# Layer L2 of a four-layer attention kernel: scores from projected queries and raw keys, with the key bias carried by the fully connected product and brought as a row by two transfers

## What is computed

```python
q = x3 @ Wq + bq                  # 256 -> 256
k = ctx @ Wk + bk                 # 128 -> 256
v = ctx @ Wv + bv
scores = softmax(q @ k.T / 16)    # per batch entry, 128 x 128
x4 = x3 + scores @ v
# fc before it:  x3 = x2 + layernorm(x2) @ fc_W + fc_b  (gain and bias of the norm folded in)
```

## Time and profile before

| | |
|---|---|
| median of 3 runs | 590.14 us (589.99 to 591.93) |
| the profiled execution, its own time | 591.77 us |
| its span from first to last instruction | 590.0 us |
| PE busy | 98% |
| POOL, DVE, ACT busy | 86%, 78%, 76% |
| granted TensorE clock, mean | 0.995 |
| DMA | mean 75 GB/s |

### The profile page before, as it was taken

The page is one execution under the profiler, slowest core; times in us unless marked ns, Lnnn a source line. Parts: engine busy times, 40 slices in busy tenths (PEclk is TensorE's granted clock), DMA queues, the critical chain, the costliest instruction groups (busy, mean ns, idle before and its releaser), DMA issues.

```text
span 590.0 us, 16396 instructions
## 1 busy us (share of the span) xinstructions
PE 576.3 (98%) x4752; PEld 562.4 (95%) x4752; DVE 461.0 (78%) x1442; ACT 449.5 (76%) x1534; POOL 505.6 (86%) x704
## 2 busy tenths in 40 slices
PE   6999999999999999999999999999999999999995
PEld 6898999999999999999999999999999999999984
DVE  2486888996888878887887779778778778967975
ACT  4679878678697777977985977968788888686663
POOL 5889999799898969988897899898959979994763
PEclk9899999999999999999999999999999999999999
DMA  8961112121312132221122224112230110000012
GB/s 255 367 209 37 56 46 92 46 77 61 98 47 82 46 106 85 82 63 65 47 64 64 72 62 138 46 28 94 70 100 11 56 46 20 2 3 0 21 36 91
DMA packets 29799, 44.06 MB, mean 75 GB/s; under 512 B 2704, under 2 KB 21520, under 8 KB 29712
## 3 DMA queue, kind: packets, MB, share of 16 engines
q1 hardware_dynamic: 29712, 43.02, 22.4%
HBM read 34.62 MB, written 8.39 MB: 73 GB/s over the span
## 4 chain that ended last, share of the span: by engine, by line
PE 90%; DVE 4%; issue 2%; ACT 1%; DMA 1%; SPq 1%; DVEq 0%; ACTq 0%
PE bank L689 15%; PE bank L696 10%; PE bank L672 9%; PE bank L702 9%; PE bank L680 7%; PE bank L713 5%; PE bank L715 5%; PE bank L714 5%; PE bank L818 5%; PE bank L840 5%; PE bank L730 4%; PE bank L802 3%; PE bank L803 2%; PE bank L804 2%; PE bank L831 1%
## 5 line engine op out<-in xcount | busy, mean ns | idle before, releaser
L961 ACT ACTIVATE prob_L<-bank,neg_max_L 128x128 f32<-128x128 f32 x320 | 115.2, 382 | 26.2 <-DVE neg_max_L L1254 24.3
L1254 DVE TENSOR_REDUCE neg_max_L<-bank 128x2 f32<-128x256 f32 (+1 forms) x128 | 61.1, 480 | 20.1 <-PE bank L696 12.7
L961 ACT ACTIVATION_READ_ACCUMULATOR prob_L<-bank,neg_max_L 128x1 f32 x320 | 70.4, 220 | 0.0
L885 ACT ACTIVATE xT_hi_L<-bank 128x512 fp32r<-128x512 f32 (+1 forms) x96 | 57.9, 606 | 15.0 <-PE bank L672 13.0
L1103 DVE TENSOR_TENSOR oT_lo_L<-bank,oT_hi_L 128x256 fp32r<-128x256 f32 (+1 forms) x96 | 47.7, 502 | 15.9 <-ACT oT_hi_L L885 15.5
L1425 POOL TENSOR_TENSOR rstd_ln<-var_eps_ln,minus_half 128x2 f32<-128x2 f32 x64 | 45.4, 710 | 16.6 <-ACT var_eps_ln L971 16.5
L885 ACT ACTIVATE probT_L<-bank 128x256 f32<-128x256 f32 (+1 forms) x96 | 43.8, 475 | 10.4 <-PE bank L680 8.2
L885 ACT ACTIVATE oT_hi_L<-bank 128x256 fp32r<-128x256 f32 (+1 forms) x96 | 44.7, 475 | 8.9 <-PE bank L702 6.4
L1103 DVE TENSOR_TENSOR xT_lo_L<-bank,xT_hi_L 128x512 fp32r<-128x512 f32 x64 | 43.4, 680 | 9.7 <-ACT xT_hi_L L885 9.4
L1484 POOL TENSOR_TENSOR x_bias<-x,bias_L 128x512 f32<-128x512 f32 x32 | 41.0, 1285 | 9.2 <-DVE x L1281 8.8
L1217 DVE BATCH_NORM_STATS2 stats_ln<-x 128x6 f32<-128x256 f32 x128 | 47.6, 413 | 0.2
(11 more groups left out here) (225 smaller groups left out, 2338.0 us busy)
## 6 DMA issues: line engine op xcount, KB each, us to landing
x_in<-in_x SPq DMA_DIRECT2D x32, 512.0 KB, 3.6
ctx_in<-in_ctx SPq DMA_DIRECT2D x32, 256.0 KB, 2.7
out<-y SPq DMA_DIRECT2D x32, 256.0 KB, 2.2
side_in<-in_side SPq DMA_DIRECT2D x32, 128.0 KB, 2.0
WqT_L<-in_L_WqT SPq DMA_DIRECT2D x3, 256.0 KB, 4.3
Wo_L<-in_L_Wo SPq DMA_DIRECT2D x2, 256.0 KB, 6.9
WkT_L<-in_L_WkT SPq DMA_DIRECT2D x3, 128.0 KB, 4.8
Wo_L1v<-in_L1v_Wo SPq DMA_DIRECT2D x1, 256.0 KB, 5.5
```

The lines of the kernel that those rows point to most:

```text
L885: activation(to, of, ACT.Copy).then_inc(done[step], 1)
L961: last = activation(at(prob[k], g)[:, b, :], block(bank, b), ACT.Exp, bias=at(neg_max[k], g)[:, b:b + 1], accum_out=at(total[k], g)[:, b:b ...
L1254: dve.tensor_reduce(at(neg_max[k], g)[:], scores, AX.X, ALU.max, negate=True).then_inc(done[f"max_{k}"], 1)
```

## The change

L2 is computed like the other layers: its queries are projected to the 128 context features, and scores are taken against the raw transposed context.

- `B2`, `b2`, `k_bias2` and the six `B2` buffers are gone. `hi_L2` now writes fp32r, a new `lo_L2` on DVE gives the rest (128x512), a new `Q_L2` on PE makes 6 fp32r matmuls, a new `q_L2` on ACT copies 128x256.
- `S_L2` has one f32 matmul 128x128 for each batch entry (4 instructions), and then one fp32r matmul over 256 columns whose stationary operand `two_ones` has ones in its first two rows and zeros elsewhere, and whose moving operand `s_row` has in its first two rows the row of key-bias terms (hi and lo).
- The key-bias term `x3 @ c` with `c = Wq @ bk / 16` is taken out of the fc product: `F_hi` and `F_lo` get two more columns (258 instead of 256), one with `fc_centred @ c` (`Fc_L2`) and one with `c` itself (`c_L2`).
- Since 2 x 258 columns don't fit one bank, `OUT_fc` is split in `OUT_fc0` and `OUT_fc1`, with a bank each, and so is `out_fc`. Each of the two DVE steps first makes one more instruction of 128x1 that forms `s_col` from the two added columns.
- `split_s` (DVE): a copy 128x2 and a difference 128x2, with a wait between them. `send_s` (SP) writes the four numbers of each partition to DRAM, `fetch_s` (SP) waits for that and reads them back as two rows of 256. The wait for it stands in `S_L2` between the score matmuls and the last one.
- Preparations: `M_L2` goes the way of the other layers, `row_k_L2` (two f32 matmuls of 256 columns), `rep_L2`, `c_L2` and `Fc_L2` are new, `M0_L1a` and `M0_L1v` are folded into `M1_L1a` and `M1_L1v`, some memsets are added.
- The order tables `STARTS` and `PREPARATIONS` are new throughout, `COPIES` gives some small tiles and `x1`, `x2`, `x3`, `x4`, `qT`, `prob` another buffer.

```diff
@@ TensorE
-            def B2_of(g):
-                pe.wait_ge(done["lo_ctx"], g + 1)
...
-                for e in range(T):
-                    for n, (w, c) in enumerate(((M2T_hi, hi), (M2T_lo, hi), (M2T_hi, lo))):
-                        last = mm(bank[:, e * TOK:(e + 1) * TOK], w[:, e * P:(e + 1) * P], c[:], start=n == 0, stop=n == 2)
-                last.then_inc(done["B2"], 1)
...
+            def OUT_fc_of(b):
+                def of(g):
...
+                    pe.wait_ge(done["lo_fc"], g + 1)
+                    to, s = bank_for(pe, f"OUT_fc{b}", g)[:, 0:D + 2], slice(b * P, (b + 1) * P)
...
+            def Q_L2(g):
+                pe.wait_ge(done["lo_L2"], g + 1)
...
+                queries("L2", g)
 
             def S_L2(g):
-                pe.wait_ge(done["b2"], g + 1)
-                pe.wait_ge(done["hi_L2"], g + 1)
+                pe.wait_ge(done["q_L2"], g + 1)
                 bank = bank_for(pe, "S_L2", g)
                 for b in range(GROUP):
-                    s = slice(b * P, (b + 1) * P)
-                    for e in range(T):
-                        last = mm(bank[:, s], at(B2, g)[:, e, s], at(xT_hi["L2"], g)[:, e, s], start=e == 0, stop=e == T - 1)
-                last.then_inc(done["S_L2"], 1)
+                    mm(block(bank, b), block(ctxT(g), b), block(at(qT["L2"], g), b), start=b == 0, stop=False, skip_group_check=True)
+                pe.wait_ge(at(fetched, g), 16 * (g // len(s_row) + 1))
+                mm(bank[:, 0:TOK], two_ones[:], at(s_row, g)[:], start=False, stop=True, skip_group_check=True).then_inc(done["S_L2"], 1)
@@ ScalarE
-            def b2(g):
...
-                for e in range(T):
-                    last = activation(at(B2, g)[:, e, :], bank_of("B2", g)[:, e * TOK:(e + 1) * TOK], ACT.Identity,
-                                      bias=k_bias2[:, e:e + 1])
-                last.then_inc(done["b2"], 1)
+            def q_L2(g):
+                act.wait_ge(done["Q_L2"], g + 1)
+                earlier(act, "S_L2", g, len(qT["L2"]))
+                copied(at(qT["L2"], g)[:], bank_of("Q_L2", g)[:, 0:TOK], "q_L2")
@@ VectorE
+            def out_fc_of(b):
+                def of(g):
...
+                    dve.wait_ge(done[f"OUT_fc{b}"], g + 1)
...
+                    bank, scale = bank_of(f"OUT_fc{b}", g), at(rstd["lnf"], g)[:, b:b + 1]
+                    dve.tensor_scalar(at(s_col, g)[:, b:b + 1], bank[:, D:D + 1], scale, bank[:, D + 1:D + 2], ALU.mult, ALU.add).then_inc(done[f"s{b}_L2"], 1)
+                    dve.scalar_tensor_tensor(out=at(x3, g)[:, b, :], in0=bank[:, 0:D], scalar=scale, in1=at(x2_bias, g)[:, b, :],
+                                             op0=ALU.mult, op1=ALU.add).then_inc(done[f"out_fc{b}"], 1)
+                return of
+
+            def split_s(g):
+                dve.wait_ge(done["s0_L2"], g + 1)
+                dve.wait_ge(done["s1_L2"], g + 1)
+                if g >= len(s_split):
+                    dve.wait_ge(at(sent, g), 16 * (g // len(s_split)))
+                dve.tensor_copy(at(s_split, g)[:, 0, :], at(s_col, g)[:]).then_inc(done["hi_s"], 1)
+                dve.wait_ge(done["hi_s"], g + 1)
+                dve.tensor_tensor(at(s_split, g)[:, 1, :], at(s_col, g)[:], at(s_split, g)[:, 0, :].bitcast(F32),
+                                  ALU.subtract).then_inc(done["split_s"], 1)
@@ SyncE
+            def send_s(g):
+
+                sp.wait_ge(done["split_s"], g + 1)
+                sp.dma_start(s_rows[g].rearrange("h (b p) -> p h b", p=P), at(s_split, g)[:].bitcast(F32),
+                             allow_slow_non_contiguous=True).then_inc(at(sent, g), 16)
+
+            def fetch_s(g):
+                sp.wait_ge(at(sent, g), 16 * (g // len(s_split) + 1))
+                if g < len(s_row):
+                    prepared(sp, "constants")
+                earlier(sp, "S_L2", g, len(s_row))
+                sp.dma_start(at(s_row, g)[0:2, :].bitcast(F32), s_rows[g]).then_inc(at(fetched, g), 16)
@@ preparations
+            def row_k_L2():
+
+                prepared(pe, "rep_L2")
                 pe.wait_ge(weights["L2_qk"], TWO)
-                bank = bank_for(pe, "M_L2")
+                bank = bank_for(pe, "row_k_L2")
                 for h in range(T):
-                    last = mm(bank[:, 0:D], w["WkT"][:, h, :], w["WqT"][:, h, :], start=h == 0, stop=h == T - 1)
-                last.then_inc(done["M_L2"], 1)
+                    last = mm(bank[:, 0:D], rep["L2"]["bk"][:, h, :], stage["L2"]["WqT"][:, h, :], start=h == 0, stop=h == T - 1)
+                last.then_inc(done["row_k_L2"], 1)
...
+            def Fc_L2():
+
+                prepared(dve, "row_k_L2")
+                dve.wait_ge(done["centred_fc"], times["centred_fc"])
+                row = bank_of("row_k_L2")[:, 0:D]
+                before = smalls(1)
+                dve.tensor_tensor(fc_times_c[:], fc_centred[:, :, 0:D], row.unsqueeze(1).to_broadcast([P, T, D]), ALU.mult).then_inc(done["small"], 1)
+                dve.wait_ge(done["small"], before + 1)
+                dve.tensor_reduce(fc_centred[:, :, D], fc_times_c[:], AX.X, ALU.add).then_inc(done["Fc_L2"], 1)
```

More of the change, by code:

```diff
@@ new lines @@
+    "fetch_s": [6421, 8104, 10088, 10538, 11770, 14279, 14802, 17778, 18827, 21009, 22330, 24617, 25105, 26684, 29165, 31514,
[7 rows of a table added]
+}
+PREPARATIONS = {"run_up": 300, "M_L2": 1751, "k_L2": 1507, "row_k_L2": 1376, "M_L0": 833, "m_L0": 1010, "N_L0": 2262, "n_L0": 2015, "M_L1a":
[14 rows of a table added]
+COPIES = {"x_in": 3, "x_bias": 3, "x2_bias": 2, "ctx_in": 10, "side_in": 3, "keys": 3, "keysT": 2, "x1": 4, "x2": 3, "xhat_ln1": 2,
[5 rows of a table added]
+    "oT_lo_L3": 1, "stats_keys": 3, "mean_var_keys": 3, "var_eps_keys": 3, "rstd_keys": 3, "stats_ln1": 3, "mean_var_ln1": 3,
+    "var_eps_ln1": 3, "rstd_ln1": 3, "stats_lnf": 3, "mean_var_lnf": 3, "var_eps_lnf": 3, "rstd_lnf": 3, "stats_ln2": 3,
+    "mean_var_ln2": 3, "var_eps_ln2": 3, "rstd_ln2": 3, "ctxT_hi": 2, "ctxT_lo": 1, "x1_bias": 3, "shift_ln2": 2, "V2": 3,
+    "s_split": 2, "s_col": 2, "s_row": 2, "xT_lo_L2": 1, "qT_L2": 1}
@@ L252 @@
 ROWS = ["L0_bo", "L1a_bo", "L1v_bo", "L3_bo", "fc_bias", "L2_bv", "L3_b1", "L3_g1", "L1a_g2", "L1a_b2", "L1v_g2", "L1v_b2"]
-EMPTIED_BY = {"T_keys": "t_keys", "B2": "b2", "Q_L0": "q_L0", "S_L0": "exp_L0", "PT_L0": "pT_L0", "O_L0": "oT_lo_L0",
+EMPTIED_BY = {"T_keys": "t_keys", "Q_L0": "q_L0", "S_L0": "exp_L0", "PT_L0": "pT_L0", "O_L0": "oT_lo_L0",
               "OUT_L0": "out_L0", "T_L1": "lo_L1", "Q_L1": "q_L1", "S_L1": "exp_L1", "PT_L1": "pT_L1",
[1 row of a table removed]
+              "O_L1": "oT_lo_L1", "OUT_L1": "out_L1", "T_fc": "lo_fc", "OUT_fc0": "out_fc0", "OUT_fc1": "out_fc1", "T_L2": "lo_L2",
+              "Q_L2": "q_L2",
               "S_L2": "exp_L2", "V_L2": "v_L2", "OUT_L2": "out_L2", "T_L3": "lo_L3", "Q_L3": "q_L3",
@@ L415, in build @@
                   for w in ("x", "ctx", "side")}
+        sent = [stack.enter_context(nc.semaphore(f"s_sent_{i}")) for i in range(COPIES["s_split"])]
+        fetched = [stack.enter_context(nc.semaphore(f"s_fetched_{i}")) for i in range(COPIES["s_row"])]
         stored = [stack.enter_context(nc.semaphore(f"stored_{i}")) for i in range(COPIES["y"])]
@@ L1269, in oT_lo_of, with lo_of @@
                 return of
-            def lo_of(k, used_by):
+            def lo_of(k, *used_by):
                 def of(g):
                     dve.wait_ge(done[f"hi_{k}"], g + 1)
-                    earlier(dve, used_by, g, len(xT_lo[k]))
+                    for step in used_by:
+                        earlier(dve, step, g, len(xT_lo[k]))
                     less(flat(at(xT_lo[k], g)), bank_of(f"T_{k}", g)[:], flat(at(xT_hi[k], g)), f"lo_{k}")
@@ L1360, in constants @@
                     pool.memset(tile[:], eps)
+                for row in s_row:
+                    pool.memset(row[:].bitcast(F32), 0.0)
+                pool.memset(two_ones[:].bitcast(F32), 0.0).then_inc(done["zeroed"], 1)
+                pool.wait_ge(done["zeroed"], 2)
+                pool.memset(two_ones[0:2, :].bitcast(F32), 1.0)
                 pool.memset(minus_half[:], -0.5).then_inc(done["constants"], 1)
@@ L1373, in replicated, with rep_L2 @@
                 return of
+            def rep_L2():
+                prepared(pool, "scaled")
+                for h in range(T):
+                    last = pool.tensor_copy(rep["L2"]["bk"][:, h, :], col("L2_bk", h, scaled_cols).to_broadcast([P, P]))
+                last.then_inc(done["rep_L2"], 1)
             def wk_gained(a):
@@ L1422, in of @@
                     pool.wait_ge(done[f"eps_{k}"], g + 1)
-                    earlier(pool, used_by, g, len(rstd[k]))
+                    for step in used_by:
+                        earlier(pool, step, g, len(rstd[k]))
                     n = rstd[k][0].shape[1]
```

214 lines of the change are left out of this document (96 added, 118 removed), and 367 rows, old and new, of tables (COPIES, EMPTIED_BY, PREPARATIONS, STARTS).

## The result

The changed kernel takes 766.2 us (median of 4 runs, 761.6 to 771.3) where the kernel before takes 591.0 beside it: a ratio of 1.296, 95% interval 1.285 to 1.307. The prediction was 582.2 us with a range up to 592.0. The forecast has the wrong sign and misses by 184 us.

The account below looks back on a forecast made before the run. PE, busy for 576.3 of 590.0 us, was taken to bound the kernel. The terms -10.4 + 0.35 + 0.6 + 0 + 1 + 0.5 = -7.95 us, from the median 590.14, gave 582.2 us, range 578.5 to 592.

Parts of the forecast that it names:

- S_L2's own price: S_L2 on PE: 0.56 us from start to start, 0.325 us less in each of 32 groups, -10.4 us.
- Rival (3): In S_L2: the matmul with the row costs like the two it replaces, 0.44 us; 592.6 us, chance 0.05.
- The transfers: send_s and fetch_s ahead of S_L2's last matmul: 3.0 and 2.2 us, chain 7.5 us against 7.7 and up.
- The term of +0.5 us for the waits: PE's wait for the row in S_L2: shortfall over the groups, taken as +0.5 us.
- rival (1): PE's wait in S_L2: the row comes too late, chain 10.5 us, stops of 17 us, 599 us; chance 0.13.
- Loads are issued long before use, so the second costs nothing: On SP's queue: loads behind a fetch wait for the send, priced at nothing.
- DVE: the sum: DVE's added work: 1.3 us a group, 42 us in all, from 461 to about 503 us.
- what DVE's queue puts back on PE: PE's waits for later answers from DVE: +1 us, bounds 0 and 5.
- Rival (2): DVE too full, 92% in stretches: waits over all layers, 5 to 8 us, say 587.5 us; chance 0.15.
- The ends: First 60 and last 30 us of the kernel: change taken as nil, kept at -2 to +2 us.
- PE's own sum: PE's changed instructions together: -9.4 us, from S_L2 -10.4, wider fc matmuls +0.35 and preparations +0.6.

Follow-up runs that it names:

- unread: The changed kernel with both transfers still made, but PE's matmul reads a row of zeros and doesn't wait for them: 685.4 us, 1.158 of before.
- no_split: The changed kernel without both transfers and without the four small DVE instructions for s in each group: 588.6 us, 0.995 of before.

## Why the prediction was wrong, step by step

- **S_L2's own price: right, slightly high.** PE in order of time, kernel without transfers, from the last fc matmul:
```profile
222.56 0.29 PE L826 MATMUL bank<-F_hi,xT_lo_fc 128*128 128x258 f32 x1
222.68 0.61 PE L845 MATMUL bank<-qT_L,ctx_in 128*128 128x128 f32 x4
223.05 0.37 PE L847 MATMUL bank<-s_row,two_ones 128*128 128x256 f32 x1
223.25 0.61 PE L730 MATMUL bank<-ctx_in,qT_L 128*128 128x128 f32 x4
```
0.57 us from start to start, forecast 0.56, and the fc matmul 0.12 apart. The row's matmul takes 0.20, not 0.12, and the four in front of it 0.37, not 0.445. Summed over all groups S_L2 goes from 28.0 to 18.9 us: 9.1 saved, 10.4 forecast. Rival (3) is out.
- **The transfers: the failed step.** The prediction's "it lies between 2.0 and 4.8" bounded send_s by rows of which none is a store of pieces this small, and 3.0 was taken. It measured 8.8, the fetch up to PE's matmul 3.05 where 2.2 was taken, and the chain came to 14.4 us instead of 7.5, longer than the median cover of 10.7. The term of +0.5 us for the waits became 104.1 with 49.8 of clock. So rival (1) was right in its mechanism and priced at 599 where 766 came. What the Trainium skill says of one descriptor for each element ("DMA: Bandwidth & Descriptors", Rules for kernel authors) was named and then given no term; the number of pieces is not what costs, though, since 512 of them 64 bytes apart take 1.9 us.
- **"Loads are issued long before use, so the second costs nothing": wrong.** In `unread` this alone, the sends ahead of loads on the DMA engines and the fetches on SP's queue, costs 85 us: 56 for the sends, the rest for the fetches. This term was put at nothing, and it is the second part of the failed step.
- **The clock had no term.** A PE wait was priced at its own length. With 104.1 us of waits for the row came 49.8 us of slower matmuls.
- **DVE: the sum right, its price wrong.** 506.6 us against 503 forecast. But s_col takes 278 ns, not 159, and what DVE's queue puts back on PE, taken as +1 with a bound of 5, is 10.5 us for the small instructions alone. Rival (2) held as well; its 587.5 would be 592 with that.
- **The ends, taken at nil.** PE's first large product waits 4.1 us for POOL's xT_lo in the kernel without transfers (1.4 before), and its granted clock in the first 60 us is 0.94 against 0.97 (0.89 in `no_split` and after): 2.7 us of wait and 0.03 x 60 = 1.8 of clock, 4.5 where the bound was 2. The wait is in every trace of the new order (3.2 to 5.0 us); the clock differs from execution to execution of one kernel (means of 0.988 to 0.999 in the kernel before), so its 1.8 is an estimate from one execution of each.

Without transfers and small instructions the kernel is 2.3 us faster than before, where PE's own sum promised about 8. I put the difference down to DVE's remaining 0.68 us a group and the start; no run separates the two in this order.

## What to carry to other kernels

Where PE is at 98%, a saving on PE is only as good as the queues that it is bought with. Small instructions added to DVE cost over a third of their length in one order here (10.5 of 28 us) and three quarters in the other (21 of 28), and a PE wait costs one and a half times its own length. An operation whose form the trace doesn't show can't be bounded by rows of another form; one probe of the store would have told that it takes 9 us. A transposing store should keep its pieces in HBM apart or at 16 bytes and more, or stay in SBUF.

## What the runs showed of the hardware

- A store of four-byte pieces side by side into HBM lands after 6 to 9 us from 64 pieces on; such pieces 64 bytes apart, or written into SBUF, after 1.9 to 2.0.
- The packets of such a store have ended 1.5 us after its issue at the median, and its landing is told 8.8 us after it.
- A load issued while such a store is under way can land behind it: 10.7 us for 128 KB instead of 2.0, with no semaphore between them.
- PE's granted clock had a mean of 0.912 in a kernel that waits for the row in 27 of 32 groups, 104.1 us in all, and 0.992 in the kernel without the transfers.
